# Attention and experts on one core: the normalised input as two fp16 parts, turned by transfers

## The reference

```python
x = x + attn_a(layernorm(x))   # x: 32 x 256 x 128; biases on q, k, v; two scores masked
x = x + ffn(layernorm(x))      # gate on the mean over tokens, top 2 of 8, gelu
x = x + attn_b(layernorm(x))   # scale 1/sqrt(128), no biases
x = x + ffn(layernorm(x))
# attention: q, k, v = xn @ W (+ b); softmax(q k^T) @ v per head; @ Wo
```

## Time and profile before

| | |
|---|---|
| time, median of 3 runs | 932.47 us (931.51 to 935.1) |
| profiled execution: its time, its span | 931.88 us, 930.1 us |
| mean granted TensorE clock | 0.986 |
| TensorE matmul, busy | 861.5 us (93%) |
| VectorE, busy | 781.5 us (84%) |
| ScalarE, busy | 757.5 us (81%) |
| GpSimd, busy | 539.8 us (58%) |
| chain that ended last | TensorE 66%, VectorE 18%, issue 8% |

### The profile page before, as it was taken

One profiled execution on the slowest core, in us unless ns is written; L12 is line 12 of the kernel. 1 busy time (PEld: TensorE's weight loads), 2 busy tenths in 40 slices (PEclk: granted clock), 3 DMA queues, 4 the chain that ended last, 5 costly groups with the idle time before them and its releaser, 6 DMA issues.

```text
span 930.1 us, 32135 instructions
## 1 busy us (share of the span) xinstructions
PE 861.5 (93%) x12592; PEld 444.0 (48%) x12592; DVE 781.5 (84%) x1410; ACT 757.5 (81%) x1305; POOL 539.8 (58%) x1086
## 2 busy tenths in 40 slices
PE   3699999999999999999999999999999999998875
PEld 1244444444445454455545445455554554554434
DVE  2889999999998989989898998989889888889533
ACT  2278888888888888888988898888898888897864
POOL 7345555545664766647565674657576485653432
PEclk9989999999999999999999999999999999999987
DMA  3354233222222222212222221222223133132001
GB/s 107 119 159 142 79 89 102 83 74 67 78 78 76 60 80 68 83 50 80 78 72 70 66 83 58 83 66 82 59 71 99 47 102 95 54 104 64 4 24 46
DMA packets 89862, 72.16 MB, mean 78 GB/s; under 512 B 5040, under 2 KB 72784, under 8 KB 89680
## 3 DMA queue, kind: packets, MB, share of 16 engines
q1 hardware_dynamic: 89280, 69.52, 24.8%
q10 hardware_dynamic: 432, 0.59, 0.2%
HBM read 39.68 MB, written 29.88 MB: 75 GB/s over the span
## 4 chain that ended last, share of the span: by engine, by line
PE 66%; DVE 18%; issue 8%; ACT 4%; POOL 2%; DMA 1%; POOLq 0%; SPq 0%; DVEq 0%; ACTq 0%
PE values_bank L829 19%; DVE nmax L643 14%; PE ring L840 11%; PE ring L850 10%; PE m_bank L816 9%; PE m_bank L977 4%; PE m_bank L1010 3%; PE ring L880 3%; PE ring L903 3%; ACT probs L717 2%; PE m_bank L950 1%; PE ring L895 1%; DMA wb<-in_attn_b 0%; DVE x L631 0%; DVE x L678 0%
## 5 line engine op out<-in xcount | busy, mean ns | idle before, releaser
L643 DVE TENSOR_REDUCE nmax<-ring 128x4 f32<-128x1024 f32 x512 | 603.7, 1216 | 46.6 <-PE ring L840 44.5
L717 ACT ACTIVATE probs<-ring 128x1024 f32<-128x1024 f32 x512 | 520.7, 1034 | 35.6 <-PE ring L850 32.9
L829 PE MATMUL values_bank<-probs,values 128*32 128x256 f32 x4096 | 277.0, 384 | 1.7 <-ACT probs L717 1.7
L850 PE MATMUL ring<-q_stack,k_stack 32*128 32x256 f16 x2048 | 198.4, 273 | 14.1 <-DVE nmax L643 14.0
L537 POOL TENSOR_SCALAR xy<-x,mv,rstd 128x128 f32<-128x128 f32 x256 | 201.7, 798 | 7.9
L840 PE MATMUL ring<-k_stack,q_stack 32*128 32x256 f16 x2048 | 183.2, 277 | 15.3 <-DMA k_stack<-scratch 5.1
L515 POOL TENSOR_SCALAR mparts<-nmax 128x32 f16<-128x32 f32 x64 | 14.1, 220 | 279.1 <-DVE nmax L643 279.0
L829 PEld LDWEIGHTS values_bank<-probs,values 128*32 128x32 f32 x4096 | 123.9, 109 | 63.8 <-issue 23.8
L850 PEld LDWEIGHTS ring<-q_stack,k_stack 32*128 32x128 f16 x2048 | 64.4, 92 | 132.7 <-issue 73.7
L840 PEld LDWEIGHTS ring<-k_stack,q_stack 32*128 32x128 f16 x2048 | 52.9, 93 | 115.4 <-ACT probs L717 41.2
L781 ACT COPY values<-m_bank 128x128 f32<-128x128 f32 x128 | 28.9, 278 | 60.3 <-PE m_bank L816 59.0
(11 more groups left out here) (118 smaller groups left out, 959.7 us busy)
## 6 DMA issues: line engine op xcount, KB each, us to landing
scratch<-parts SPq DMA_DIRECT2D x384, 64.0 KB
q_stack<-scratch SPq DMA_DIRECT2D x64, 256.0 KB, 2.6
k_stack<-scratch SPq DMA_DIRECT2D x64, 256.0 KB, 3.0
out<-x SPq DMA_DIRECT2D x16, 256.0 KB, 3.0
x<-in_x SPq DMA_DIRECT2D x3, 768.0 KB, 6.5
q_stack<-maxT SPq DMA_DIRECT2D x128, 8.0 KB
x<-in_x SPq DMA_DIRECT2D x1, 896.0 KB, 6.7
x<-in_x SPq DMA_DIRECT2D x1, 640.0 KB, 5.3
```

The lines of the kernel that those rows point to most:

```text
L643: nc.vector.tensor_reduce(dst, src, axis=AX.X, op=ALU.max, negate=True).then_inc(max_done, 1)
L717: nc.scalar.activation(probs[g % 2][:, c:c + 2, :, :], pair_of("exps", n, p)[:, :, :].rearrange("p x (k q) -> p x k q", k=TILES), ACT.Exp) ...
L829: last = nc.tensor.matmul(values_bank[32 * c:32 * (c + 1), a * TOKENS:(a + 1) * TOKENS], values[turn % RING][:, k, PER_GROUP * g + c, :], ...
L850: last = nc.tensor.matmul(pair_of("exps", turn, p)[:, a, k * TOKENS:(k + 1) * TOKENS], k_stack[r][rows, of // 2, k * P:(k + 1) * P], q_sta ...
```

## The change

The normalised tiles of the attention are no longer turned by TensorE. GpSimd scales 1/sqrt by 2^8, and splits the attention's half of `xy` into two fp16 parts, `xn`, with two more operations. SyncE turns the four tiles (two parts, two tiles) by transposing transfers into `xnT`, now a ring of four buffers. q, k and v are projected as three fp16 products (`PRODUCTS`: high with high, high with low, low with high) of full 128-column weights; the weights are split into `w_parts` in the opening, after being scaled to a common level by powers of two, now for v as well; the scales are undone in ScalarE's copies and in Wo. The maxima's parts are padded to 128 columns and turned by two transposing transfers from `mparts` to `maxT`; SyncE waits for these to land and then issues the two row transfers as before. TensorE's transposes L950 and half of L1010, and ScalarE's copies L724 and L794, are gone. The experts' normalised tiles are still turned by TensorE.

```diff
-        xnT = [sb(f"xnT{i}", [P, TOKENS]) for i in range(2)]
+        xn = [sb(f"xn{i}", [P, 2, TILES, WIDTH], FP16) for i in range(2)]
+        xnT = [sb(f"xnT{i}", [P, 2, TOKENS], FP16) for i in range(RING)]
+        w_parts = [sb(f"w_parts{i}", [P, 2, 3 * WIDTH], FP16) for i in range(2)]
...
-        mparts = [sb(f"mparts{i}", [P, TILES, MAX_PARTS * HEADS], FP16) for i in range(2)]
-        maxT = [sb(f"maxT{i}", [MAX_PARTS * HEADS, TOKENS], FP16) for i in range(2)]
+        mparts = [sb(f"mparts{i}", [P, TILES, P], FP16) for i in range(2)]
+        maxT = [sb(f"maxT{i}", [P, TOKENS], FP16) for i in range(2)]
...
-            for c, w in enumerate((wa[:, 0:WIDTH], wa[:, WIDTH:2 * WIDTH], wb[:, 0:WIDTH], wb[:, WIDTH:2 * WIDTH])):
-                last = nc.scalar.activation(onT[:, 0:WIDTH], w, ACT.Square, scale=float(WIDTH) ** 0.5, accum_out=norms[:, c:c + 1])
+            for c, w in enumerate(m[:, i * WIDTH:(i + 1) * WIDTH] for m in (wa, wb) for i in range(3)):
+                last = nc.scalar.activation(onT[:, 0:WIDTH], w, ACT.Square, scale=float(WIDTH) ** 0.5, accum_out=norms[:, c // 3, c % 3:c % 3 + 1])
...
-            nc.scalar.copy(identh[:, :], ident[:, :])
...
+            for m in mparts:
+                nc.gpsimd.memset(m[:, :, MAX_PARTS * HEADS:], 0.0)
...
-            dve.wait_ge(squares_done, 4)
+            dve.wait_ge(squares_done, 6)
...
+            to_q = (float(HEAD) ** -0.5, float(WIDTH) ** -0.5)
+            for b, w in enumerate((wa, wb)):
...
+                then(nc.vector.tensor_scalar(w[:, 3 * WIDTH:4 * WIDTH], w[:, 3 * WIDTH:4 * WIDTH], factor[:, b, BACK_V:BACK_V + 1], None, ALU.mult))
+                then(nc.vector.tensor_copy(w_parts[b][:, 0, :], w[:, 0:3 * WIDTH]))
+                nc.vector.tensor_tensor(w_parts[b][:, 1, :], w[:, 0:3 * WIDTH], w_parts[b][:, 0, :], ALU.subtract).then_inc(weights_ready, 1)
+                dve.wait_ge(weights_ready, b + 1)
...
-                        sp.wait_ge(maxT_ready, (n + 1) + 1)
+                        sp.wait_ge(mparts_ready, (n + 1) + 1)
+                        if live(n - 1):
+                            sp.wait_ge(max_in[(n - 1) % 2], (n - 1) // 2 * 32 + 32)
+                        for t in range(TILES):
+                            sp.dma_start(maxT[(n + 1) % 2][:, t * P:(t + 1) * P], mparts[(n + 1) % 2][:, t, :], transpose=True).then_inc(maxT_in[(n + 1) % 2], 16)
+                        sp.wait_ge(maxT_in[(n + 1) % 2], (n + 1) // 2 * 32 + 32)
                         for part in range(MAX_PARTS):
                             dst = q_stack[(n + 1) % RING][MAX_ROW + part::BLOCK, :, :]
                             sp.dma_start(dst, maxT[(n + 1) % 2][HEADS * part:HEADS * (part + 1), :]).then_inc(max_in[(n + 1) % 2], 16)
+                    if live(n + 5):
+
+                        sp.wait_ge(xn_ready, (n + 5) + 1)
+                        if live(n + 1):
+                            sp.wait_ge(v_done, (n + 1) + 1)
+                        for part in range(2):
+                            for t in range(TILES):
+                                sp.dma_start(xnT[(n + 5) % RING][:, part, t * P:(t + 1) * P], xn[(n + 5) % 2][:, part, t, :],
+                                             transpose=True).then_inc(xnT_in[(n + 5) % 2], 16)
                     if live(n + 4):
...
-                            pool.wait_ge(mT_done, (n - 1) + 1)
+                            pool.wait_ge(maxT_in[(n - 1) % 2], (n - 1) // 2 * 32 + 32)
                         pool.wait_ge(max_done, (n + 1) * PAIRS + PAIRS)
...
-                        if norm_steps(n) > 2:
-                            pool.wait_ge(xyT_done, norm_steps(n - 2))
+                        if live(n - 5):
+                            pool.wait_ge(yT_done, (n - 5) + 1)
                         for m, turn in ((0, n + 5), (1, n - 3)):
                             for t in range(TILES):
                                 if live(turn):
                                     last = nc.gpsimd.tensor_scalar(xy[i][:, m, t, :], x[:, (turn % ITEMS) * TILES + t, :], mv[i][:, m, t, 0:1],
                                                                    rstd[i][:, m, t:t + 1], ALU.subtract, ALU.mult)
                         last.then_inc(xy_ready, 1)
+                        if live(n + 5):
+                            if live(n + 3):
+                                pool.wait_ge(xnT_in[(n + 3) % 2], (n + 3) // 2 * 64 + 64)
+                            pool.wait_ge(xy_ready, norm_steps(n))
+                            nc.gpsimd.tensor_scalar(xn[i][:, 0, :, :], xy[i][:, 0, :, :], 1.0, 0.0, ALU.mult, ALU.add).then_inc(xhi_done, 1)
+                            pool.wait_ge(xhi_done, (n + 5) + 1)
+                            nc.gpsimd.tensor_tensor(xn[i][:, 1, :, :], xy[i][:, 0, :, :], xn[i][:, 0, :, :], ALU.subtract).then_inc(xn_ready, 1)
...
-                    if p == 0 and live(n + 1):
-                        act.wait_ge(mT_done, (n + 1) + 1)
-                        if live(n - 1):
-                            act.wait_ge(max_in[(n - 1) % 2], (n - 1) // 2 * 32 + 32)
-                        nc.scalar.copy(maxT[(n + 1) % 2][:, :],
-                                       m_bank[:, :].bitcast(FP16)[0:MAX_PARTS * HEADS, 0:TOKENS]).then_inc(maxT_ready, 1)
...
-                            nc.scalar.activation(qk32[i][:, 0, :], src[:, 0, :], ACT.Identity, bias=bqs[:, :])
-                            last = nc.scalar.activation(qk32[i][:, 1, :], src[:, 1, :], ACT.Identity, bias=bks[:, :])
+                            nc.scalar.activation(qk32[i][:, 0, :], src[:, 0, :], ACT.Identity, bias=bqs[:, :], scale=same)
+                            last = nc.scalar.activation(qk32[i][:, 1, :], src[:, 1, :], ACT.Identity, bias=bks[:, :], scale=same)
...
-                    if p == 5 and (live(n + 5) or live(n - 3)):
-                        act.wait_ge(xyT_done, norm_steps(n))
-                        if live(n + 5):
-                            nc.scalar.copy(xnT[(n + 5) % 2][:, :], m_bank[:, 0:TOKENS]).then_inc(xnT_ready, 1)
-                        if live(n - 3):
-                            item = (n - 3) % ITEMS
-                            nc.scalar.activation(normT[:, item:item + 1, :], m_bank[:, TOKENS:2 * TOKENS].unsqueeze(1), ACT.Copy,
-                                                 accum_out=pooled[:, item:item + 1]).then_inc(yT_ready, 1)
+                    if p == 5 and live(n - 3):
+                        act.wait_ge(yT_done, (n - 3) + 1)
+                        item = (n - 3) % ITEMS
+                        nc.scalar.activation(normT[:, item:item + 1, :], m_bank[:, 0:TOKENS].unsqueeze(1), ACT.Copy, scale=2.0 ** -UP,
+                                             accum_out=pooled[:, item:item + 1]).then_inc(yT_ready, 1)
...
-                    if p == 1 and live(n + 1):
-                        if batch_at(n, 2) is None and batch_at(n, 3) is None:
-                            fill_m(pe, maxT_ready, (n + 1) + 1)
-                        pe.wait_ge(mparts_ready, (n + 1) + 1)
-                        for t in range(TILES):
-                            last = nc.tensor.transpose(m_bank[:, :].bitcast(FP16)[0:MAX_PARTS * HEADS, t * P:(t + 1) * P],
-                                                       mparts[(n + 1) % 2][:, t, :], identh[:, :])
-                        last.then_inc(mT_done, 1)
...
-                        wq, wk = projections[(n + 4) // ITEMS][0:2]
+                        parts_w, parts_x = w_parts[(n + 4) // ITEMS], xnT[(n + 4) % RING]
                         fill_m(pe, qk32_ready, (n + 4) + 1)
-                        if n + 4 == 0:
-                            pe.wait_ge(weights_ready, 1)
-                        pe.wait_ge(xnT_ready, (n + 4) + 1)
-                        for a, wmat in enumerate((wq, wk)):
-                            last = by_columns(m_bank[:, a * TOKENS:(a + 1) * TOKENS], wmat, xnT[(n + 4) % 2][:, :],
-                                              start=(a == 0), stop=(a == 1))
+                        if n + 4 in (0, ITEMS):
+                            pe.wait_ge(weights_ready, (n + 4) // ITEMS + 1)
+                        pe.wait_ge(xnT_in[(n + 4) % 2], (n + 4) // 2 * 64 + 64)
+                        for a in range(2):
+                            for k, (w, h) in enumerate(PRODUCTS):
+                                last = nc.tensor.matmul(m_bank[:, a * TOKENS:(a + 1) * TOKENS], parts_w[:, w, a * WIDTH:(a + 1) * WIDTH], parts_x[:, h, :],
+                                                        start=(a == 0 and k == 0), stop=(a == 1 and k == len(PRODUCTS) - 1), skip_group_check=True)
                         last.then_inc(qk_done, 1)
...
-                        wv = projections[(n + 3) // ITEMS][2]
+                        parts_w, parts_x = w_parts[(n + 3) // ITEMS], xnT[(n + 3) % RING]
                         fill_m(pe, v_ready, (n + 3) + 1)
                         for t in range(TILES):
```

(31 more changed lines are left out.)

59 lines of the change are left out of this document (30 added, 29 removed).

## The result

The changed kernel takes **1230.59 us** (1230.05 to 1233.51), against 933.26 for the kernel before beside it: a ratio of 1.319, 95% interval 1.316 to 1.323. The profiled execution has a span of 1228.7 us, 298.6 more than before.

A forecast was written before the change was run, and what follows sets the result against it. TensorE bounds the kernel by a little; SyncE's serial queue would take over. Its loop adds 55.5 us over 61 steps, the opening 7.5, the end takes off 5: 931.9 + 58 = 990 us, range 895 to 1200.

The forecast's parts named there:

- c: SyncE's issue of one transposing transfer, six per step: taken as 0.558 us, within bounds of 0.326 to 1.703.
- a transpose costs far more: Rival on SyncE's queue: transposing issues cost up to 1.703 us each, giving 1200 to near 1420 us; chance 0.15.
- L: SyncE's wait per step until the maxima have landed after their second transposing transfer: taken as 2.5 us.
- The base of the loop: SyncE's existing issues and landing wait per step, without waits on other engines: taken as 8.3 us.
- The loop of 14.15: SyncE's serial time per step after the change: 8.3 base, 3.35 for six issues, 2.5 for landing.
- The end: After the last load: the last step loses SyncE's spare 4.9 us, so 5 us less.
- The opening's two rounds: Two more rounds of SyncE's own loop in the opening: 2.23 us more each, 4.5 us of the opening's 7.5.
- Issues above 1.1 us, which would put the time over the range: Sign of a wrong forecast on SyncE's queue: transposing issues above 1.1 us, putting the time over the range.
- TensorE's gain: TensorE's saving per step: 0.16 maxima transposes, 0.29 input transposes, 0.31 q and k, 0.76 us in sum.
- What of it shows: Part of TensorE's saving that shortens a plain step, VectorE's 11.33 us becoming the floor: 0.5 us, at most 0.91.
- The rival of 901 us: Rival: SyncE is not the bound, so TensorE's 34 us show, less 3 in the opening; chance 0.28.
- The scales ride on instructions that are there already: nothing: ScalarE's copies: multiplying in the scales would add no time.

The follow-up runs named there:

- the run with idle turns: Kernel before, with SyncE also issuing six transposing transfers of 128x128 per step that nobody reads or waits for: 1162.45 us, ratio 1.242.
- the run with the maxima on TensorE: Changed kernel with maxima turned by TensorE and copied by ScalarE, input turned by one merged transfer, no scales in q and k copies: 941.61 us, ratio 1.008.

## Why the prediction was wrong

The direction, held at 0.65, and the mechanism were right: SyncE's serial queue becomes the bound, by the sum of its issues and landings. The time, 990 us in a range of 895 to 1200, was wrong by 241 us. By its own steps:

- **The step that failed is c, the issue of a transposing transfer.** I took 0.558, the rows of maxima, as "nearest in kind"; it is 1.23 us in the median. In the mean of whole blocks the six of a step take 2.53 (the two of the maxima) and 5.25 (the four of the input), 7.78 us in place of 3.35, and 8.05 in the run with idle turns, or 1.34 each. The prediction's case "a transpose costs far more", held at 0.15, gave 1200 us at c = 1.12; with 1.23 to 1.35 it was the case that came. The choice by likeness was the error: the trace had no transposing transfer, the bounds were 0.326 to 1.703, and I set the value in the lower third of them, by the shape of the data. The runs show that shape and size don't matter to the issue.
- The Trainium skill, VectorE: DVE Perf Modes, section "The three transpose paths", gives 1309 ns for a 128x128 transpose by transfer in bf16, which the prediction did not weigh. The trace agrees with it, for fp16, as the price of the queue in a row of issues (1.31 us each in the changed kernel's blocks of four); until the data has landed it is 2.4 us.
- **L**, the landing after the second transpose, was taken at 2.5 and is 1.30 in the mean. This error of 1.2 us per step went the other way.
- The base of the loop, 8.3, held roughly: 18.01 - 1.30 - 7.78 = 8.93. The loop of 14.15 with the errors of c, L and the base is then 14.15 + 4.43 - 1.20 + 0.63 = 18.01. The end held: 5 us less were predicted, 6.4 came. The opening's two rounds got 4.7 us each where 2.23 stood, the same c; in all the opening was 14.0 for 7.5.
- What was to be seen: GpSimd's wait left SyncE's list, the maxima's landing came onto it, shorter than the 2 us named, steps don't grow with bursts, and the opening's rounds are in series. "Issues above 1.1 us, which would put the time over the range" is what happened. Other signs didn't come: TensorE was to be released by a transfer at its first score, and waits at the projection; its busy time was to fall by 40 us, and rose with the lower clock; VectorE's was to stay, and rose from 781.5 to 800.6.
- **TensorE's gain** of 0.76 us per step, 34 us in all, was to sit idle, and did, though not in front of a stack load: TensorE waits for the turned input. Its size can be read at a clock of 1.00, in a plain step of the run with the maxima on TensorE (rows of q and k below, before and in that run). Busy time of q and k falls from 1.07 to 0.83 us, where 0.31 less was forecast; that of V falls from 0.65 to 0.51, where nothing was; that of the transposes falls from 0.66 to 0.44, where 0.29 was. That is 0.60 in sum, as forecast, with errors that cancel by luck. But busy time of the whole step, in which overlapping records count once, falls only from 12.12 to 11.85, and the step from 12.24 to 12.19. "What of it shows", 0.5 us in a plain step (0.35 with the maxima on TensorE, as expected for that run), was the term that failed here. The rival of 901 us, held at 0.28, was reached by no run.
- **"The scales ride on instructions that are there already: nothing"** was wrong. ScalarE's rows, with the scale read from a tile, are below; the same copies took 0.477 and 0.591 us before. That makes 8 of the 28 us by which ScalarE's busy time fell less than forecast (17.6 us for 46); the rest stays open.
- **GpSimd** was well sized (0.407 + 0.671 = 1.08 us for 1.2), but not free: it is late in the last bursts, which the two steps of the earlier trace rows didn't show.

TensorE's instructions of q and k (timeline), in the kernel before and in the run with the maxima on TensorE:

```profile
146.04 1.07 PE L816 MATMUL m_bank<-xnT,wa 128*32 128x256 f32 x16
```

```profile
134.82 0.83 PE L999 MATMUL m_bank<-xnT,w_parts 128*128 128x256 f16 x6
```

Groups by line, ScalarE and GpSimd of the changed kernel:

```profile
L791 ACT ACTIVATE qk<-m_bank,factor 128x512 f32<-128x512 f32 x32 | 22.0, 687 | 77.2 <-PE m_bank L989 77.2
...
L788 ACT ACTIVATE qk<-m_bank,bqs,factor 128x256 f32<-128x256 f32 x32 | 18.1, 565 | 120.7 <-PE m_bank L989 120.7
```

```profile
L579 POOL TENSOR_TENSOR xn<-xy,xn 128x256 f16<-128x256 f32 x64 | 42.9, 671 | 5.3
...
L577 POOL TENSOR_SCALAR xn<-xy 128x256 f16<-128x256 f32 x64 | 26.1, 407 | 10.1 <-POOL xy L570 9.9
```

## What to carry to other kernels

A queue that issues transfers is an engine with a busy time of its own: add up its issues and the landings it waits for, per step, before giving it more. Count transposing transfers by instruction, 1.1 to 1.35 us each here whatever their size, and turn several tiles with one; then place it inside a landing wait that the queue has anyway, but not behind a wait for something that is needed later than its own data. And where engines stand in a ring, 0.3 us of busy time off one of them may be worth nothing, while 1.1 us more on an engine that is idle for 40% of the span can still cost some in the steps where it has the most to do.

## What the runs showed of the hardware

- One at a time, each waited for, a transposing transfer from on-chip memory to on-chip memory takes SyncE 1.09 to 1.22 us to issue for 16x128 as for 128x512 of fp16; a plain one of 128x128 took 0.47 to 0.56.
- Issued back to back, some take 2 to 3.2 us: the mean in a block of six was 1.34 us with a median of 1.23.
- A scale read from a tile in place of none adds about 0.09 us to a ScalarE copy of 256 or 512 columns.
